# Second attention of a two-layer block: its stages one slot closer together, and the small VectorE steps at other places in a slot

## The chip, the cores and the metric

The kernel runs on one core of a Trainium2 chip. The time is that of one execution on the device, in microseconds (us). The engines are named PE (TensorE), DVE (VectorE), ACT (ScalarE), POOL (GpSimd) and SP (SyncE, which here only issues DMAs).

## The reference

A block of two layers over x of 4 x 1024 tokens by 128. Around two attentions stand four feed-forward layers. The change is in the second attention, which computes two softened sums for each head and adds them:

```python
Q, K, V = (proj(Wq, bq), proj(Wk, bk), proj(Wv, bv))
S = jnp.einsum('bhnd,bhmd->bhnm', Q, K) / dh ** 0.5
W_tau = jax.nn.softmax(S, axis=-1)
W_sigma = 1.0 / ((1.0 + jnp.abs(S) / b_) ** 2 + t_ ** 2)
W_sigma = W_sigma / W_sigma.sum(axis=-1, keepdims=True)
tau = jnp.einsum('bhnm,bhmd->bhnd', W_tau, V)...
sigma = jnp.einsum('bhnm,bhmd->bhnd', W_sigma, V)...
f = 0.5 * tau + 0.5 * sigma
y = f @ Wo.T + bo
```

There are 4 batches of 16 heads, so 64 heads of 1024 x 1024 scores with 8 values a token.

## The kernel before

The function `attend_both` runs through the 64 heads in 256 slots. A head takes four slots; a slot holds two tiles (i = 0 and 1) of 128 rows by 1024 scores. It is a pipeline written out by hand: in slot j each engine works on the slots j, j - LS, j - LT and so on, and the lags LS, LT, LE, LP say how far behind the maxima each stage stands. Sixteen slots are unrolled in the body of a loop. The order on an engine is the order of the code in its `body(it, j)`; engines meet by semaphores alone.

What the engines do in slot j:

- PE computes scores into the PSUM tiles `pm` (for the row maxima, slot j), `pb` (for tau, slot j - LT) and `pa` (for sigma, slot j - LS), each two matmuls of 512 columns at L1951. `weigh` (L1969) multiplies finished weights by the values, eight matmuls, and sums a head in `po`. Once a head the eight columns of maxima are turned into rows (L2011), and the evicted `po` is turned in four pieces (L2026); both go to the PSUM tile `ptr`.
- DVE takes the maximum of `pm` (L2119), the absolute value of `pa` into the SBUF tile `sg` (L2130, an AND on the bits), for i = 0 and i = 1. Then it squares the last quarter of `sg` (L2137: (|s| + b) |s|, both inputs in SBUF). Once a head `negated` writes minus the turned maxima as two bfloat16 rows (L2080, then L2083, both read `ptr`), which SP sends by DMA into the stack of Q (L1924), so that the tau scores come out with their maximum subtracted. And once a head `output` takes reciprocals (L2097), multiplies (L2102, `ptr` by `rz` into `fw`) and adds (L2106, two slices of `fw` into F, which lies in the tile `XNT`; both inputs and the output are in SBUF).
- POOL squares the first three quarters of `sg`: L1898 (tensor_scalar, `sg` + b into `shifted`, which lies in the tile `f0w`) and L1901 (tensor_tensor, `sg` times `shifted`). L1898 waits until both absolute values of its slot are done.
- ACT computes exp for tau (L2044, twice a slot), then for sigma the logarithm (L2053) and the exponential of its negative (L2057), and once a head it evicts `po` into `osb` (L2063).

At the start the sigma work of the slots 0 to 3 is done early, in slots 0 to 3; in the slots from 4 to LS + 3 only maxima (and from slot LT on tau) are done. The tau scores of a head wait for its rows of maxima.

The wait that ties POOL to DVE, and DVE's last steps in a slot:

```python
pool.wait_ge(abs_done, 2 * s + 2)
...
nc.vector.scalar_tensor_tensor(buf[:, :, CUT:T], buf[:, :, CUT:T],
                               parh[:, ring(j, ls), 0:1], buf[:, :, CUT:T],
                               ALU.add, ALU.mult).then_inc(sq_dve, 1)
...
negated(it, j, 0, 1)
output(it, j, 2, LP + 3)
```

Of the kernel before, what the change touches and what calls it, by code (L numbers as in the profile page):

```python
# [15 lines left out]
P = 128  # L16
# [5 lines left out]
HEADS = B * H  # L22
# [1774 lines left out]
def attend_both(nc, tag, V, F, par, qd, kd, ident, stacks, scratch, stack_in):  # L1797
# [5 lines left out]
    SLOTS = HEADS * TT // 2  # L1803
    PER = TT // 2
    UNROLL = PER * RING
    LS, LT, LE, LP = 5, 7, 7, 8
    EARLY = 4
    SC = DH ** -0.5
    CUT = 49 * T // 64
# [1 line left out]
    with ExitStack() as ctx:  # L1811
# [55 lines left out]
        def slots(eng, body):  # L1867
            for j in range(UNROLL):
                body(0, j)
            with eng.Fori(1, SLOTS // UNROLL) as it:  # L1870
                for j in range(UNROLL):
                    body(it, j)
            for j in range(LP + 4):
                body(SLOTS // UNROLL, j)

        def some(x, least=1):
# [3 lines left out]
        with nc.Block() as block:  # L1880
# [64 lines left out]
            @block.tensor  # L1945
            def _(pe):
                pe.wait_ge(vh_cleared, 1)

                def scores(out, lhsT, rhs, t, rows_, sem):
                    for lo in range(0, T, CH):  # L1950
                        last = nc.tensor.matmul(out[:, lo:lo + CH], lhsT[0:rows_, t * P:(t + 1) * P],  # L1951
                                                rhs[0:rows_, lo:lo + CH], start=True, stop=True)
                    last.then_inc(sem, 1)

                def weigh(it, j, s, i):

                    lag = LP + i
                    h, k, r = head(it, j, lag), (j - lag) % PER, (j - lag) % 4
                    t = 2 * k + i
                    if i == 0:  # L1960
                        pe.wait_ge(tau_exp, 2 * s + 2)
                        pe.wait_ge(sig_done, s + 1)
                    if t == 0:
                        pe.wait_ge(head_in[ring(j, lag)], HEAD_LOADS * rounds(it, j, lag))
                        if some(h):
                            pe.wait_ge(o_sb, h)
                    values = Vh[:, ring(j, lag), t * (DH + 1):t * (DH + 1) + 32]
                    for q, (wts, half) in enumerate(((pt[r], 0), (pt[r], 1), (sg[r], 0), (sg[r], 1))):
                        last = nc.tensor.matmul(po[32 * q:32 * q + 32, :], values,  # L1969
                                                wts[:, i, half * CH:(half + 1) * CH],  # L1970
                                                start=(t == 0), stop=(t == TT - 1))
                    last.then_inc(pv_done, 1)

                def body(it, j):
                    sm, st = at(it, j, 0), at(it, j, LT)
                    ss, ls = at_sigma(it, j, LS, 0)
                    rm, rs, rt = (((j - lag) // PER) % RING for lag in (0, ls, LT))
                    if sm is not None and j % PER == 0:
                        pe.wait_ge(stack_in[rm], STACK_LOADS * (it + 1))
                    if st is not None and (j - LT) % PER == 0:  # L1980
                        pe.wait_ge(rows_in[rt], ROW_LOADS * rounds(it, j, LT))
                    for i in range(2):
                        if sm is not None:
                            top = pm
                            if not spare_abs(it, j):
                                if some(2 * sm + i):
                                    pe.wait_ge(max_red, 2 * sm + i)
                            elif j > EARLY:
                                pe.wait_ge(max_red, 2 * sm + i - 1)
                                top = (pm, pa)[i]  # L1990
                            elif i == 0:
                                pe.wait_ge(max_red, 2 * sm)
                            else:
                                pe.wait_ge(abs_done, 2 * EARLY)
                                top = pa
                            scores(top, Q[rm], K[rm], 2 * (j % PER) + i, 96, max_mm)
                        if st is not None:
                            if some(2 * st + i):
                                pe.wait_ge(tau_exp, 2 * st + i)
                            scores(pb, K[rt], Q[rt], 2 * ((j - LT) % PER) + i, P, tau_mm)  # L2000
                        if ss is not None:
                            if some(2 * ss + i):
                                pe.wait_ge(abs_done, 2 * ss + i)
                            scores(pa, K[rs], Q[rs], 2 * ((j - ls) % PER) + i, 96, abs_mm)
                        if i == 1 and j % PER == 0 and at(it, j, 1) is not None:

                            h = head(it, j, 1)
                            pe.wait_ge(max_red, TT * h + TT)
                            if some(h, 3):
                                pe.wait_ge(f_done, h - 2)  # L2010
                            nc.tensor.transpose(ptr[0:TT, 0:P], mx[:, ((j - 1) // PER) % 2, :], ident[:])\  # L2011
                                .then_inc(rows_turned, 1)
                        sp_ = at(it, j, LP + 1 - i)
                        if sp_ is not None:
                            weigh(it, j, sp_, 1 - i)
                    if (j - LP - 2) % PER == PER - 1 and at(it, j, LP + 2) is not None:

                        h = head(it, j, LP + 2)
                        pe.wait_ge(o_sb, h + 1)
                        if isinstance(h, int) and h + 3 > HEADS:  # L2020
                            pe.wait_ge(rows_sb, HEADS)
                            pe.wait_ge(f_done, h)
                        else:
                            pe.wait_ge(rows_sb, h + 3)
                        for c in range(4):
                            last = nc.tensor.transpose(ptr[:, c * P:(c + 1) * P], osb[:, c * P:(c + 1) * P],  # L2026
                                                       ident[:])
                        last.then_inc(o_turned, 1)

                slots(pe, body)  # L2030

            @block.scalar
# [35 lines left out]
            def _(dve):  # L2068
# [40 lines left out]
                def body(it, j):  # L2109
                    sm = at(it, j, 0)  # L2110
                    ss, ls = at_sigma(it, j, LS, 0)
                    for i in range(2):
                        if sm is not None:
                            top = pa if i == 1 and spare_abs(it, j) else pm
                            t = 2 * (j % PER) + i
                            dve.wait_ge(max_mm, 2 * sm + i + 1)
                            if i == 0 and j % PER == 0 and some(sm, 2 * PER):
                                dve.wait_ge(rows_turned, head(it, j, 0) - 1)
                            nc.vector.tensor_reduce(mx[:, (j // PER) % 2, t:t + 1], top[:], AX.X, ALU.max)\  # L2119
                                .then_inc(max_red, 1)  # L2120
                        if i == 0:
                            negated(it, j, 1, 2)
                            output(it, j, 0, LP + 3)
                        else:
                            output(it, j, 1, LP + 3)
                        if ss is not None:
                            dve.wait_ge(abs_mm, 2 * ss + i + 1)
                            if some(ss, 4):
                                dve.wait_ge(pv_done, 2 * (ss - 4) + i + 1)
                            nc.vector.tensor_scalar(sg[(j - ls) % 4][:, i, :].bitcast(I32), pa[:].bitcast(I32),  # L2130
                                                    SIGN_OFF, None, ALU.bitwise_and).then_inc(abs_done, 1)
                    if ss is not None:
                        buf = sg[(j - ls) % 4]
                        dve.wait_ge(abs_done, 2 * ss + 2)
                        if (j - ls) % PER == 0:
                            dve.wait_ge(head_in[ring(j, ls)], HEAD_LOADS * rounds(it, j, ls))
                        nc.vector.scalar_tensor_tensor(buf[:, :, CUT:T], buf[:, :, CUT:T],  # L2137
                                                       parh[:, ring(j, ls), 0:1], buf[:, :, CUT:T],
                                                       ALU.add, ALU.mult).then_inc(sq_dve, 1)
                    negated(it, j, 0, 1)  # L2140
                    output(it, j, 2, LP + 3)

                slots(dve, body)
        m.clear_sems()
# [155 lines left out]
```

## Time and profile before

| | |
|---|---|
| time before, median of 3 runs | 2910.45 us (2909.16 to 2911.09) |
| the profiled execution | 2910.0 us, of which the span 2908.2 us |
| PE, DVE busy over the span | 2446.8 us (84%), 2437.5 us (84%) |
| ACT, POOL busy over the span | 2255.8 us (78%), 1998.7 us (69%) |
| second attention | first maximum at 1156.35 us, last add at 2633.88 us |

The span is the time from the first to the last instruction of one profiled execution. Busy times are sums of the recorded instructions of an engine; on ACT and DVE a record can overlap its neighbour by some hundredths to some tenths of a microsecond, since the next instruction is already let in. So the time that an instruction costs its engine is the distance from its start to the start of the next, and the record's length is the time until its result is there.

### The profile page before, as it was taken

How to read it: one execution, taken by the hardware profiler on the slowest of the kernel's cores; microseconds unless marked ns; L12 is line 12 of the kernel's file. 1: busy time of each engine (PE TensorE's matmuls, PEld its weight loads, DVE VectorE, ACT ScalarE, POOL GpSimd, SP SyncE). 2: the span in 40 equal slices, each digit the busy share in tenths (PEclk: the TensorE clock that was granted, in tenths of full speed). 3: DMA queues.
4: the chain of work that ended last, by engine and by line, in shares of the span. 5: the costliest groups of instructions: out<-in, count | busy, mean ns of one | idle time of the engine just before them, and what ended most of it. 6: DMA issues, size and time to landing. Idle time of an engine off the chain costs nothing. (4 is left out here: it accounts for less than half of the span.)

```text
span 2908.2 us, 60009 instructions
## 1 busy us (share of the span) xinstructions
PE 2446.8 (84%) x18487; PEld 1013.1 (35%) x18614; DVE 2437.5 (84%) x3916; ACT 2255.8 (78%) x2521; POOL 1998.7 (69%) x1255
## 2 busy tenths in 40 slices
PE   2657999998577996899998999999999999983898
PEld 2643333334465663122222222222222222222566
DVE  4667888885577656999999999999999999986765
ACT  4464777776455555799999999999999999992554
POOL 4532222222454654799999999999999999993455
PEclk9977999999687997799999999999999999996799
DMA  3232100000120002000000000000000000000000
GB/s 117 70 92 71 29 29 28 28 29 8 50 81 1 1 0 100 15 15 15 14 18 14 14 14 16 16 14 14 15 17 14 14 14 17 15 1 1 1 11 18
DMA packets 93503, 76.57 MB, mean 26 GB/s; under 512 B 32480, under 2 KB 73960, under 8 KB 93264
## 3 DMA queue, kind: packets, MB, share of 16 engines
q1 hardware_dynamic: 89104, 66.36, 7.8%
q0 software_dynamic: 4288, 8.82, 0.9%
q8 instruction: 58, 0.95, 0.1%
q14 instruction: 53, 0.43, 0.1%
HBM read 47.77 MB, written 24.42 MB: 25 GB/s over the span
## 5 line engine op out<-in xcount | busy, mean ns | idle before, releaser
L1901 POOL TENSOR_TENSOR a_sg<-a_sg,all_f0w 128x1568 f32<-128x1568 f32 x256 | 904.9, 3535 | 21.4
L2044 ACT ACTIVATE a_pt<-a_pb 128x1024 f32<-128x1024 f32 x512 | 702.7, 1372 | 12.1 <-PE a_pb L1951 12.1
L2119 DVE TENSOR_REDUCE a_mx<-a_pm 128x1 f32<-128x1024 f32 x507 | 613.8, 1211 | 11.4 <-PE a_pm L1951 10.0
L2130 DVE TENSOR_SCALAR a_sg<-a_pa 128x1024 int32<-128x1024 int32 x512 | 615.6, 1202 | 8.5 <-PE a_pa L1951 8.3
L2053 ACT ACTIVATE a_sg<-a_sg,a_parh 128x2048 f32<-128x2048 f32 x256 | 602.2, 2352 | 15.3 <-POOL a_sg L1901 15.3
L1969 PE MATMUL a_po<-a_pt,a_Vh 128*32 128x512 f32 x2048 | 541.2, 607 | 64.7 <-ACT a_osb L2063 62.5
L2057 ACT ACTIVATE a_sg<-a_sg 128x2048 f32<-128x2048 f32 x256 | 581.2, 2270 | 0.1
L1969 PE MATMUL a_po<-a_sg,a_Vh 128*32 128x512 f32 x2048 | 541.1, 607 | 0.0
L1898 POOL TENSOR_SCALAR all_f0w<-a_sg,a_parh 128x1568 f32<-128x1568 f32 x256 | 513.6, 2006 | 30.0 <-DVE a_sg L2130 27.1
L1711 ACT ACTIVATE a_pt<-a_ring 128x1024 f32<-128x1024 f32 (+2 forms) x384 | 313.6, 846 | 150.4 <-PE a_ring L1638 147.1
L1783 DVE TENSOR_REDUCE a_mx<-a_ring 128x2 f32<-128x1024 f32 (+3 forms) x384 | 359.1, 955 | 74.0 <-PE a_ring L1621 55.1
L1951 PE MATMUL a_pm<-all_K,all_Q 96*128 96x512 bf16 x1014 | 312.2, 390 | 44.9 <-DVE a_mx L2119 33.8
L1552 POOL TENSOR_SCALAR_AFFINE_SELECT a_pt<-a_pt 128x256 f32<-128x256 f32 x256 | 104.0, 406 | 355.6 <-ACT a_pt L1711 355.2
L1951 PE MATMUL a_pa<-all_Q,all_K 96*128 96x512 bf16 x1024 | 311.1, 385 | 10.5 <-DVE a_sg L2130 1.5
L1951 PE MATMUL a_pb<-all_Q,all_K 128*128 128x512 bf16 x897 | 281.1, 383 | 28.0 <-ACT a_pt L2044 17.7
L2137 DVE SCALAR_TENSOR_TENSOR a_sg<-a_sg,a_parh 128x480 f32<-128x480 f32 x256 | 218.7, 854 | 10.6
L1951 PEld LDWEIGHTS a_pm<-all_K,all_Q 96*128 96x128 bf16 x1014 | 63.1, 98 | 428.2 <-DVE a_mx L2119 362.3
L895 ACT ACTIVATE f_sg<-f_psg 128x512 f32<-128x512 f32 x176 | 104.5, 594 | 117.1 <-PE f_psg L854 117.1
L1655 PE MATMUL a_po<-a_pt,a_Vh 128*32 128x384 f32 (+3 forms) x1920 | 191.4, 437 | 1.9 <-POOL a_pt L1552 1.8
L1969 PEld LDWEIGHTS a_po<-a_pt,a_Vh 128*32 128x32 f32 x2048 | 75.9, 108 | 280.4 <-issue 260.6
L949 DVE TENSOR_TENSOR f_su<-f_psu,f_sg 128x512 f32<-128x512 f32 x144 | 98.7, 687 | 79.4 <-PE f_psu L854 74.0
L1638 PE MATMUL a_ring<-all_Q,all_K 50*128 50x512 bf16 (+2 forms) x768 | 132.1, 342 | 37.9 <-DVE a_mx L1783 33.1
(283 smaller groups left out, 4585.2 us busy)
## 6 DMA issues: line engine op xcount, KB each, us to landing
all_Q<-q_parts SPq DMA_DIRECT2D x256, 48.0 KB
all_K<-k_parts SPq DMA_DIRECT2D x256, 48.0 KB
k_parts<-p_parts SPq DMA_DIRECT2D x16, 384.0 KB, 3.1
e_recs<-routed_rows SPq DMA_DIRECT2D x70, 64.5 KB, 1.9
all_Q<-a_rows SPq DMA_DIRECT2D x256, 2.0 KB
q_parts<-p_parts SPq DMA_DIRECT2D x16, 192.0 KB, 2.4
q_parts<-p_parts SPq DMA_DIRECT2D x8, 384.0 KB, 2.6
a_Vh<-all_V SPq DMA_DIRECT2D x64, 36.0 KB, 1.8
```

The source lines that it names most:

```text
L1711: nc.scalar.activation(pt[n % 4][:, :, ga:gb, c * P:CH], of_weight(y)[:, :, 0:(gb - ga) * width].rearrange("p u (g n) -> p u g n", n=width ...
L1783: nc.vector.tensor_reduce(mx[:, j % 2, half, :, strip_at(t)], of_maximum(y)[:, :, 0:min(CH, (t + 1) * P - half * CH)], AX.X, ALU.max).then ...
L1898: nc.gpsimd.tensor_scalar(sums, buf[:, :, 0:CUT], b2, 1.0, ALU.add, ALU.mult)\
L1901: nc.gpsimd.tensor_tensor(buf[:, :, 0:CUT], buf[:, :, 0:CUT], sums, ALU.mult)\
L1951: last = nc.tensor.matmul(out[:, lo:lo + CH], lhsT[0:rows_, t * P:(t + 1) * P], rhs[0:rows_, lo:lo + CH], start=True, stop=True)
L1969: last = nc.tensor.matmul(po[32 * q:32 * q + 32, :], values, wts[:, i, half * CH:(half + 1) * CH], start=(t == 0), stop=(t == TT - 1))
L2044: nc.scalar.activation(pt[(j - LT) % 4][:, i, :], pb[:], ACT.Exp, scale=SC)\
L2053: nc.scalar.activation(buf[:], buf[:], ACT.Ln, bias=parh[:, ring(j, le), 1:2]).then_inc(ln_done, 1)
L2057: nc.scalar.activation(buf[:], buf[:], ACT.Exp, scale=-1.0).then_inc(sig_done, 1)
L2119: nc.vector.tensor_reduce(mx[:, (j // PER) % 2, t:t + 1], top[:], AX.X, ALU.max)\
L2130: nc.vector.tensor_scalar(sg[(j - ls) % 4][:, i, :].bitcast(I32), pa[:].bitcast(I32), SIGN_OFF, None, ALU.bitwise_and).then_inc(abs_done, 1)
L2137: nc.vector.scalar_tensor_tensor(buf[:, :, CUT:T], buf[:, :, CUT:T], parh[:, ring(j, ls), 0:1], buf[:, :, CUT:T], ALU.add, ALU.mult).then_ ...
```

## The change

All four lags are one slot shorter. The maxima of a head are turned on PE one half slot earlier, right behind the scores of i = 0, and the two negated rows are written behind the first and the second absolute values of that slot. The four turns of the output stand on PE ahead of a `weigh` instead of behind it. The three output steps on DVE are spread anew: the reciprocal at the end of a slot, the multiply and the add in the two halves of the next one. One slot more is run at the end, since the last output steps are one slot further behind LP.

```diff
-    LS, LT, LE, LP = 5, 7, 7, 8
+    LS, LT, LE, LP = 4, 6, 6, 7
...
-            for j in range(LP + 4):
+            for j in range(LP + 5):
                 body(SLOTS // UNROLL, j)
...
-                        if i == 1 and j % PER == 0 and at(it, j, 1) is not None:
+                        if i == 0 and j % PER == 0 and at(it, j, 1) is not None:
...
+                        if i == 0 and (j - LP - 3) % PER == PER - 1 and at(it, j, LP + 3) is not None:
+
+                            h = head(it, j, LP + 3)
+                            pe.wait_ge(o_sb, h + 1)
...
+                            for c in range(4):
+                                last = nc.tensor.transpose(ptr[:, c * P:(c + 1) * P], osb[:, c * P:(c + 1) * P],
+                                                           ident[:])
+                            last.then_inc(o_turned, 1)
                         sp_ = at(it, j, LP + 1 - i)
                         if sp_ is not None:
                             weigh(it, j, sp_, 1 - i)
-                    if (j - LP - 2) % PER == PER - 1 and at(it, j, LP + 2) is not None:
...
                         if i == 0:
-                            negated(it, j, 1, 2)
-                            output(it, j, 0, LP + 3)
+                            output(it, j, 1, LP + 4)
                         else:
-                            output(it, j, 1, LP + 3)
+                            output(it, j, 2, LP + 4)
                         if ss is not None:
                             dve.wait_ge(abs_mm, 2 * ss + i + 1)
...
                                                     SIGN_OFF, None, ALU.bitwise_and).then_inc(abs_done, 1)
+                        negated(it, j, i, 1)
...
-                    negated(it, j, 0, 1)
-                    output(it, j, 2, LP + 3)
+                    output(it, j, 0, LP + 3)
```

Line numbers of the changed kernel are one or two lower: the maximum is L2118, the absolute values L2128, the squares L2136, the reciprocal L2096, the multiply L2101, the add L2105, the negated rows L2079 and L2082, the turn of the output L2023.

On DVE, in the slot of the loop that holds the multiply, the order before is this (`a_fw` is written by the multiply and read by the add, `a_sg` by the squares):

```order
L2097 RECIPROCAL a_rz<-a_ptr 128x16
L2130 TENSOR_SCALAR a_sg<-a_pa 128x1024
L2116 REGISTER_ALU
L2119 TENSOR_REDUCE a_mx<-a_pm 128x1
L2102 TENSOR_TENSOR a_fw<-a_ptr,a_rz 128x128
L2130 TENSOR_SCALAR a_sg<-a_pa 128x1024
L2137 SCALAR_TENSOR_TENSOR a_sg<-a_sg,a_parh 128x2x240
L2106 ISA
L2106 TENSOR_TENSOR all_XNT<-a_fw 128x8x8
L2116 ISA
L2119 TENSOR_REDUCE a_mx<-a_pm 128x1
```

In the changed kernel the same slot, from the squares of the slot before to its own squares, reads:

```order
L2136 SCALAR_TENSOR_TENSOR a_sg<-a_sg,a_parh 128x2x240
L2096 RECIPROCAL a_rz<-a_ptr 128x16
L2115 ISA
L2118 TENSOR_REDUCE a_mx<-a_pm 128x1
L2101 TENSOR_TENSOR a_fw<-a_ptr,a_rz 128x128
L2128 TENSOR_SCALAR a_sg<-a_pa 128x1024
L2115 REGISTER_ALU
L2118 TENSOR_REDUCE a_mx<-a_pm 128x1
L2105 ISA
L2105 TENSOR_TENSOR all_XNT<-a_fw 128x8x8
L2128 TENSOR_SCALAR a_sg<-a_pa 128x1024
L2136 SCALAR_TENSOR_TENSOR a_sg<-a_sg,a_parh 128x2x240
```

The add stood behind the squares, with the next slot's maximum after it; it now stands between the second maximum and the second absolute values of the slot.

The first slot of a head on DVE in the changed kernel, where the maxima of the head before are turned (`a_rows` are the negated rows):

```order
L2079 TENSOR_SCALAR a_rows<-a_ptr 8x128
L2115 REGISTER_ALU
L2118 TENSOR_REDUCE a_mx<-a_pm 128x1
L2128 TENSOR_SCALAR a_sg<-a_pa 128x1024
L2082 SCALAR_TENSOR_TENSOR a_rows<-a_ptr,a_rows 8x128
L2135 ISA
L2136 SCALAR_TENSOR_TENSOR a_sg<-a_sg,a_parh 128x2x240
```

Before, L2080 stood at the end of that slot, behind the squares, and L2083 behind the first maximum of the next one; now the second row is written between the absolute values and the squares.

## Rows read from the trace of the kernel before

**Rows 1.** Windows: us, busy us of PE, PEld, DVE, ACT, POOL, clock, DMA.

```profile
1420.00:2560.00 1140.00, 1041.62 (x5825) 266.12 (x5924) 1130.15 (x1267) 1140.00 (x861) 1118.35 (x406) 1.00 0.05 15
```

**Rows 2.** Timeline of ACT: start us, length us, engine, line; two evictions in a row.

```profile
2004.46 1.01 ACT L2063 ACTIVATE a_osb<-a_po 128x512 f32<-128x512 f32 x1
...
2027.01 1.01 ACT L2063 ACTIVATE a_osb<-a_po 128x512 f32<-128x512 f32 x1
```

**Rows 3.** L2044 by its line: durations in ns, min/median/max, first and last start.

```profile
L2044 ACT ACTIVATE a_pt<-a_pb x512: 1006/1408/1457, 1187.3 to 2625.5; 128x1024 f32<-128x1024 f32 x171
```

**Rows 4.** Timeline of DVE over the slot that holds the add.

```profile
1988.31 1.20 DVE L2130 TENSOR_SCALAR a_sg<-a_pa 128x1024 int32<-128x1024 int32 x1
1989.65 0.72 DVE L2137 SCALAR_TENSOR_TENSOR a_sg<-a_sg,a_parh 128x480 f32<-128x480 f32 x1
1990.29 1.21 DVE L2119 TENSOR_REDUCE a_mx<-a_pm 128x1 f32<-128x1024 f32 x1
1991.43 0.24 DVE L2097 RECIPROCAL a_rz<-a_ptr 128x16 f32<-128x16 f32 x1
1991.59 1.16 DVE L2130 TENSOR_SCALAR a_sg<-a_pa 128x1024 int32<-128x1024 int32 x1
...
1993.80 0.27 DVE L2102 TENSOR_TENSOR a_fw<-a_ptr,a_rz 128x128 f32<-128x128 f32 x1
1993.99 1.21 DVE L2130 TENSOR_SCALAR a_sg<-a_pa 128x1024 int32<-128x1024 int32 x1
1995.24 0.72 DVE L2137 SCALAR_TENSOR_TENSOR a_sg<-a_sg,a_parh 128x480 f32<-128x480 f32 x1
1995.87 0.21 DVE L2106 TENSOR_TENSOR all_XNT<-a_fw 128x64 f32 x1
```

**Rows 5.** Timeline of POOL over the same slot.

```profile
1989.68 2.04 POOL L1898 TENSOR_SCALAR all_f0w<-a_sg,a_parh 128x1568 f32<-128x1568 f32 x1 [0.20 <-DVE a_sg L2130]
1991.81 3.52 POOL L1901 TENSOR_TENSOR a_sg<-a_sg,all_f0w 128x1568 f32<-128x1568 f32 x1
1995.37 2.07 POOL L1898 TENSOR_SCALAR all_f0w<-a_sg,a_parh 128x1568 f32<-128x1568 f32 x1
```

**Rows 6.** Timeline of DVE and POOL in the output projection: L1384 free, then beside L1344.

```profile
2648.58 0.17 DVE L1384 TENSOR_TENSOR o_t<-o_t,o_ve 128x8 f32<-128x8 f32 x1
...
2670.78 2.33 POOL L1344 TENSOR_TENSOR all_X<-all_X,all_lb 128x1024 f32<-128x1024 f32 x1
...
2670.87 2.26 DVE L1384 TENSOR_TENSOR o_t<-o_t,o_ve 128x8 f32<-128x8 f32 x1
```

**Rows 7.** Timeline near the end of the attention: L1901, and the squares beside it.

```profile
2589.19 3.51 POOL L1901 TENSOR_TENSOR a_sg<-a_sg,all_f0w 128x1568 f32<-128x1568 f32 x1
...
2591.68 1.54 DVE L2137 SCALAR_TENSOR_TENSOR a_sg<-a_sg,a_parh 128x480 f32<-128x480 f32 x1
```

**Rows 8.** L2106 and L1898 by their lines: durations in ns, min/median/max.

```profile
L2106 DVE TENSOR_TENSOR all_XNT<-a_fw x64: 212/218/224, 1229.8 to 2633.9; 128x64 f32 x60, 128x64 f32<-128x64 f32 x4
...
L1898 POOL TENSOR_SCALAR all_f0w<-a_sg,a_parh x256: 1932/1995/2077, 1161.2 to 2615.7; 128x1568 f32<-128x1568 f32 x128
```

**Rows 9.** The page's groups: busy us, mean ns, idle us before them.

```profile
L1898 POOL TENSOR_SCALAR all_f0w<-a_sg,a_parh 128x1568 f32<-128x1568 f32 x256 | 513.6, 2006 | 30.0 <-DVE a_sg L2130 27.1
```

**Rows 10.** Timeline of POOL: L1898 of slot 0 and of slot 4.

```profile
1161.23 2.02 POOL L1898 TENSOR_SCALAR all_f0w<-a_sg,a_parh 128x1568 f32<-128x1568 f32 x1 [6.01 <-DVE a_sg L2130]
...
1201.47 1.93 POOL L1898 TENSOR_SCALAR all_f0w<-a_sg,a_parh 128x1568 f32<-128x1568 f32 x1 [18.02 <-DVE a_sg L2130]
```

**Rows 11.** Timeline while the pipeline fills: the second negated row, and PE behind its DMA.

```profile
1181.93 0.27 DVE L2083 SCALAR_TENSOR_TENSOR a_rows<-a_ptr,a_rows 8x128 bf16<-8x128 f32 x1
...
1184.74 1.04 PE L1951 MATMUL a_pm<-all_K,all_Q 96*128 96x512 bf16 x2 [0.31 <-DMA all_Q<-a_rows]
```

**Rows 12.** Timeline at the end: the last L1901 and the last logarithm.

```profile
2617.73 3.54 POOL L1901 TENSOR_TENSOR a_sg<-a_sg,all_f0w 128x1568 f32<-128x1568 f32 x1
...
2623.63 2.08 ACT L2053 ACTIVATE a_sg<-a_sg,a_parh 128x2048 f32<-128x2048 f32 x1
```

More of the change, by code:

```diff
@@ L2012, in body @@
                                 .then_inc(rows_turned, 1)
+                        if i == 0 and (j - LP - 3) % PER == PER - 1 and at(it, j, LP + 3) is not None:
+                            h = head(it, j, LP + 3)
+                            pe.wait_ge(o_sb, h + 1)
+                            if isinstance(h, int) and h + 3 > HEADS:
+                                pe.wait_ge(rows_sb, HEADS)
+                                pe.wait_ge(f_done, h)
+                            else:
+                                pe.wait_ge(rows_sb, h + 3)
+                            for c in range(4):
+                                last = nc.tensor.transpose(ptr[:, c * P:(c + 1) * P], osb[:, c * P:(c + 1) * P],
+                                                           ident[:])
+                            last.then_inc(o_turned, 1)
                         sp_ = at(it, j, LP + 1 - i)
@@ L2015, in body @@
                             weigh(it, j, sp_, 1 - i)
-                    if (j - LP - 2) % PER == PER - 1 and at(it, j, LP + 2) is not None:
[L2018 to L2028, printed above, removed]
                 slots(pe, body)
```

## Prediction

> **What bounds the kernel now.** I first read the page's busy shares, which say little here since they mix ten stages, and then the stretch of the second attention by windows [rows 1]. The attention runs from about 1155 to 2634 us. Between 1420 and 2560 us, where nothing starts or ends, ACT is busy 1140.00 of 1140 us, DVE 1130.15, POOL 1118.35 and PE 1041.62, at full granted clock. Three engines are full at once, so I had to find out which one sets the pace, and how far the others may slip.
>
> ACT does. One head (four slots) takes 22.55 us from one eviction of `po` to the next [rows 2]. An exponential L2044 takes 1006 ns at its shortest and 1408 ns at its median [rows 3]; the work is the same each time, so I read the 0.4 us as waiting behind the instruction ahead. ACT is never short of work in the steady part, and small slips of the others are caught by these 0.4 us.
>
> Then DVE and POOL, row by row over one slot [rows 4, 5]. DVE has no gap: maximum, absolute values, maximum, absolute values, each 1.13 us after the last, then the squares L2137. POOL has a gap of 0.20 us once in this piece; otherwise L1901 and L1898 follow each other. L1898 waits for the second absolute values of its slot. So POOL has almost no reserve: what comes late on DVE ahead of that instruction costs POOL time.
>
> The third thing to see is how DVE and POOL block each other. In the output projection a tiny DVE instruction with both inputs in SBUF, L1384 on 128x8, took 2.26 us where 0.17 us is its free length [rows 6]. It began at 2670.87, 0.09 us after POOL's tensor_tensor L1344, and ended at 2673.13; L1344 ended at 2673.11. Such a DVE instruction waits for the end of POOL's tensor_tensor. Inside the attention the squares L2137 show it too: 0.72 us free, 1.54 us at 2591.68, ended at 2593.22, which is 0.52 us after L1901 ended at 2592.70 [rows 7]. DVE instructions that read PSUM don't wait: L2102 took 0.27 us at 1993.80 in the middle of an L1901 that lasted from 1991.81 to 1995.33 [rows 4, 5].
>
> **The change, part by part.**
>
> *The output add (L2106 before).* It adds two slices of `fw`, both in SBUF, and writes SBUF: the form that waits. Today it stands right behind the squares. There it starts at 1995.87, when L1901 has ended (1995.33), and takes 0.21 us [rows 4, 5]; over 64 instances it is 212 to 224 ns [rows 8]. The change puts it in the second half of the slot, between the maximum and the absolute values (the second piece of order in the section on the change). Where is L1901 then? In today's rows of this very slot the squares of the slot before start at 1989.65 and are followed 0.64 us later. Put in the new order from there: reciprocal 1990.29, maximum 1990.46, multiply 1991.59, absolute values 1991.79, maximum 1992.92, add 1994.05 (0.17 us for the reciprocal, 0.20 for the multiply, 1.13 for each of the others: the differences of starts in rows 4). L1901 runs from 1991.81 to 1995.33 [rows 5]. The add lands 2.2 us into it and 1.3 us before its end, further from both ends than any shift of phase seen here. It waits for the end.
>
> Behind the add, in order on DVE, stand the absolute values of this slot, and POOL's next L1898 waits for those. So POOL goes idle, and DVE cannot make it good earlier, since DVE is itself tied to the end of L1901 by the squares. The idle time of POOL per head: the absolute values start about 0.03 us around the end of L1901 (a waiting instruction ends 0.02 us after POOL's, and the next starts 0.08 us before that end, as 1990.29 behind 1989.65 + 0.72); they take 1.20 us; L1898 starts 0.17 us after their end (1989.68 against 1988.31 + 1.20) [rows 4, 5, 6]. That is 1.37 us. Absolute values stand behind the add for heads 0 to 61 (the add of head h is in slot 4h + 14, the last absolute values in slot 259): 62 x 1.37 = **+84.9 us**. Bounds for one, with 0.1 us of doubt on how closely the three follow each other: 1.25 and 1.45.
>
> *POOL's waits of today.* L1898 waited 30.0 us in all, of which 6.01 at the start and 18.02 in the filling [rows 9, 10]. The other 6.0 us are waits like the 0.20 above, ahead of the first absolute values of a head. With POOL held once a head, DVE runs ahead in the other slots and these go: **-6.0 us** (bound: nothing). L1898 is 1932 to 2077 ns [rows 8], and I take its longer records for the share of the add and the squares beside it; the add leaves it, which I estimate at 0.03 us a head: **-2 us**, between -6 and +2.
>
> *One lag less, at the start.* One slot with maxima alone goes, but the first tau scores need the row of maxima. PE waited for this DMA, then began slot 7 at 1184.74; the second half of the rows was written from 1181.93, so the way takes 2.8 us [rows 11]. In the new order it stands behind the second maximum of slot 4, one maximum (1.13 us) earlier. Slot 6, which is the first with tau scores then, begins at some 1183.6 and takes the place of slot 7: **-1.1 us**.
>
> *The end.* Today ACT is behind: the last L1901 ends at 2621.27, its logarithm starts at 2623.63 [rows 12]. With ACT no longer full it can start right then: **-2.3 us**, between 0 and -2.4.
>
> *Edits costed at nothing.* The negated rows are the same two instructions, both reading PSUM and so not held by POOL, moved by about half a slot. Outside the slot of the add DVE has over 1 us a head of slack then; without it they could cost what they last, 0.27 us each [rows 11]. The turn of the maxima and the four turns of the output on PE move ahead of a `weigh`. PE waits 98.4 of the 1140 us [rows 1], which is 1.9 us a head (50.6 heads), and gets 1.2 us more; were that cover gone, a few tenths a head would reach DVE's second maximum.
>
> *ACT as a floor.* POOL's head becomes 22.55 + 1.2 = 23.8 us, above ACT's 22.55, so nothing of the 1.37 us is hidden by ACT; PE waits too.
>
> Sum: 84.9 - 6.0 - 2 - 1.1 - 2.3 = +73.5 us. The profiled execution took 2910.0 us (span 2908.2), which gives 2983.5; the median shown is 2910.45, so 2984 against it.
>
> **A rule weighed.** In the 64 rows of L2106 POOL's L1898 is recorded as running (1995.37 to 1997.44 around 1995.87), and the add takes 0.21 us all the same [rows 4, 5, 8]. The Trainium skill, on the page SBUF — State Buffer, section "Who interferes with whom", says that a DVE instruction with two SBUF inputs contends with a GpSimd instruction that reads SBUF, and that the second to issue fully blocks. Taken by recorded starts it would make each of today's adds wait some 1.6 us, and these rows do not; by the rows the add is free behind the squares and held by L1901, and by the rule it would be held in both places, so that the change would add nothing; that outcome is rival A's. The measured rows decide for me: the squares, which start first, seem to hold POOL's L1898, and the add follows in their shelter.
>
> **The rivals.**
> *A, the add isn't held* (the change is then neutral). For: its neighbourship with L1898 cost it nothing 64 times. Against: rows 6 and 7, the same form against the same POOL instruction. Then ACT keeps the pace, and only the -1.1 us at the start is left: 2909 us. It decides where the hold is under some 0.1 us a head.
> *B, faster.* As A, and POOL's 6.0 us of waits turn into time: 2910.45 - 6.0 - 1.1 = 2903 us. Against: ACT is full [rows 1 to 3], so it cannot use them.
> *C, slower still.* The second negated row now stands between the absolute values and the squares of the first slot of a head. If L1898 gets in first and holds the squares for its own work (about 1.4 us, from the squares' end to its end: 1995.96 to 1997.44), the squares end some 1.3 us later, of which DVE's lead takes 0.3 us, and POOL loses about 1 us more a head: 2984 + 62 = 3046 us. The squares would start some 0.12 us after the absolute values, L1898 0.17 us; today one slot in 16 has 0.14 and 0.17 (1989.65 and 1989.68 against 1989.51) and the squares took 0.72 us there [rows 4, 5]. It decides where the squares start after L1898.
>
> **How the numbers follow.** The add held: 0.84. A: 0.09. B: 0.03. C: 0.04. The forecast is the first case's time, 2984 us. Its range: at the low end 62 x 1.25 - 6 - 6 - 1.1 - 2.4 = 62, at the high end 62 x 1.45 + 2 - 1.1 = 91, with the present waits kept and nothing given back at the end. On 2910 us that is 2972 to 3001, rounded to 2970 and 3000. It leaves out A, B and C, 0.16 in all, and little of the first. A change within 0.2% (5.8 us) can't be told from none in this kernel. Faster by more: B, 0.03. Within: A, 0.09. Slower: 0.88.
>
> **What the changed profile would show.** The add (L2105 then) at 1.2 to 1.6 us on average instead of 0.22, each ending within 0.1 us of an end of L1901; POOL's idle time ahead of L1898 at about 110 us, put down to DVE's absolute values; a head 23.8 us from one eviction of `po` to the next; L2043 near 1.0 us, no longer 1.4. An add of 0.22 us in the middle of L1901 makes the prediction wrong (A); squares of over 2 us once a head mean C.

## The result, and the profile after

The changed kernel takes 2982.18 us (median of 4 runs, 2977.1 to 2982.58), beside 2909.8 us for the kernel before, measured along with it (4 runs, 2907.73 to 2911.09): 1.0244 times as long, 95% interval 1.0232 to 1.0256. It is slower by 72 us. The prediction was 2984 us and slower. The profiled execution took 2981.99 us, of which the span is 2980.2 us: 72.0 us more than before in both.

The page's groups of the changed kernel (busy us, mean ns, idle us before them) show where the time stands:

```profile
L1898 POOL TENSOR_SCALAR all_f0w<-a_sg,a_parh 128x1568 f32<-128x1568 f32 x256 | 509.5, 1990 | 110.4 <-DVE a_sg L2128 107.6
L2043 ACT ACTIVATE a_pt<-a_pb 128x1024 f32<-128x1024 f32 x512 | 523.8, 1023 | 57.4 <-PE a_pb L1951 51.9
```

POOL's idle time ahead of L1898 rose from 30.0 us [rows 9] to 110.4 us. ACT's exponential fell from 1408 ns at the median [rows 3] to 1024 ns: it hardly waits behind the instruction ahead any more.

The window in the middle, with the columns of [rows 1]:

```profile
1420.00:2560.00 1140.00, 1002.88 (x5620) 259.02 (x5616) 1134.85 (x1201) 1103.96 (x817) 1057.29 (x385) 1.00 0.05 14
```

DVE's busy time even rose, 1130.15 to 1134.85 us, though it starts fewer instructions (1201 in place of 1267). The record of a held instruction counts as busy, so DVE's busy share says nothing of the work done here; the counts do. The other engines lost busy time.

The lines of the add, the squares and L1898 (ns, min/median/max; below L1898 its waits, in us and times):

```profile
L2105 DVE TENSOR_TENSOR all_XNT<-a_fw x64: 224/1520/3607, 1233.3 to 2706.7; 128x64 f32 x60, 128x64 f32<-128x64 f32 x4
...
L2136 DVE SCALAR_TENSOR_TENSOR a_sg<-a_sg,a_parh x256: 696/940/2474, 1160.7 to 2688.8; 128x480 f32<-128x480 f32 x128
...
L1898 POOL TENSOR_SCALAR all_f0w<-a_sg,a_parh x256: 1967/1982/2037, 1160.8 to 2690.7; 128x1568 f32<-128x1568 f32 x128
...
  DVE a_sg L2128: 107.6, 62
```

The add went from a median of 218 ns [rows 8] to 1520 ns. The 62 waits in the last line are not yet those of the 62 heads whose add has absolute values behind it: they hold the wait of 6.01 us at the start and the one of 18.25 us in the filling. In the timeline of POOL the other 60 are of 1.38 or 1.39 us each, and two more of the same length (2.8 us together), at the first and at the last of these heads, are put down to "issue". That makes one wait for each of the 62 heads. The slot of one add on DVE (start us, length us), which answers to [rows 4]:

```profile
1705.98 0.27 DVE L2101 TENSOR_TENSOR a_fw<-a_ptr,a_rz 128x128 f32<-128x128 f32 x1
1706.18 1.21 DVE L2128 TENSOR_SCALAR a_sg<-a_pa 128x1024 int32<-128x1024 int32 x1
1707.31 1.21 DVE L2118 TENSOR_REDUCE a_mx<-a_pm 128x1 f32<-128x1024 f32 x1
1708.44 1.51 DVE L2105 TENSOR_TENSOR all_XNT<-a_fw 128x64 f32 x1
1709.87 1.21 DVE L2128 TENSOR_SCALAR a_sg<-a_pa 128x1024 int32<-128x1024 int32 x1
1711.12 0.72 DVE L2136 SCALAR_TENSOR_TENSOR a_sg<-a_sg,a_parh 128x480 f32<-128x480 f32 x1
```

And POOL beside it, as in [rows 5]:

```profile
1706.34 3.53 POOL L1901 TENSOR_TENSOR a_sg<-a_sg,all_f0w 128x1568 f32<-128x1568 f32 x1
1711.25 2.02 POOL L1898 TENSOR_SCALAR all_f0w<-a_sg,a_parh 128x1568 f32<-128x1568 f32 x1 [1.39 <-DVE a_sg L2128]
```

The add starts 2.10 us into L1901 and ends at 1709.95, 0.08 us after L1901 (1709.87). The absolute values start at 1709.87 and end at 1711.08; L1898 starts 0.17 us later, after 1.39 us of idle. The two timelines together tell the cause: the wait is put down to the absolute values, which took their usual 1.21 us, so it is their start that is late, and what stands ahead of them is the add.

### The profile page after: what moved, and what is told of

Read it like the earlier page. It is cut to its first block and busy times, and to the rows that moved or that the text cites. A ratio compares the mean times of both kernels' runs of the same rounds, so it can differ in the third digit from the quotient of the medians.

```text
span 2980.2 us, 60091 instructions
## 1 busy us (share of the span) xinstructions
PE 2463.6 (83%) x18614; PEld 1018.0 (34%) x18614; DVE 2522.2 (85%) x3916; ACT 2283.3 (77%) x2521; POOL 1994.1 (67%) x1255
## 5 line engine op out<-in xcount | busy, mean ns | idle before, releaser
L1901 POOL TENSOR_TENSOR a_sg<-a_sg,all_f0w 128x1568 f32<-128x1568 f32 x256 | 904.5, 3533 | 21.4
L2118 DVE TENSOR_REDUCE a_mx<-a_pm 128x1 f32<-128x1024 f32 x508 | 611.2, 1203 | 13.2 <-PE a_pm L1951 13.2
L2128 DVE TENSOR_SCALAR a_sg<-a_pa 128x1024 int32<-128x1024 int32 x512 | 618.6, 1208 | 2.0 <-PE a_pa L1951 2.0
L1898 POOL TENSOR_SCALAR all_f0w<-a_sg,a_parh 128x1568 f32<-128x1568 f32 x256 | 509.5, 1990 | 110.4 <-DVE a_sg L2128 107.6
L2043 ACT ACTIVATE a_pt<-a_pb 128x1024 f32<-128x1024 f32 x512 | 523.8, 1023 | 57.4 <-PE a_pb L1951 51.9
L2052 ACT ACTIVATE a_sg<-a_sg,a_parh 128x2048 f32<-128x2048 f32 x256 | 512.2, 2001 | 15.3 <-POOL a_sg L1901 15.3
L2056 ACT ACTIVATE a_sg<-a_sg 128x2048 f32<-128x2048 f32 x256 | 487.6, 1905 | 0.1
L1951 PE MATMUL a_pb<-all_Q,all_K 128*128 128x512 bf16 x1024 | 307.6, 381 | 7.2 <-ACT a_pt L2043 7.2
L2136 DVE SCALAR_TENSOR_TENSOR a_sg<-a_sg,a_parh 128x480 f32<-128x480 f32 x256 | 226.6, 885 | 6.9
L1951 PEld LDWEIGHTS a_pa<-all_Q,all_K 96*128 96x128 bf16 x1024 | 68.8, 97 | 322.8 <-DVE a_sg L2128 313.5
```

Of the source, the lines that this page charges most:

```text
L1898: nc.gpsimd.tensor_scalar(sums, buf[:, :, 0:CUT], b2, 1.0, ALU.add, ALU.mult)\
L1901: nc.gpsimd.tensor_tensor(buf[:, :, 0:CUT], buf[:, :, 0:CUT], sums, ALU.mult)\
L2043: nc.scalar.activation(pt[(j - LT) % 4][:, i, :], pb[:], ACT.Exp, scale=SC)\
L2052: nc.scalar.activation(buf[:], buf[:], ACT.Ln, bias=parh[:, ring(j, le), 1:2]).then_inc(ln_done, 1)
L2056: nc.scalar.activation(buf[:], buf[:], ACT.Exp, scale=-1.0).then_inc(sig_done, 1)
```

## The experiments

My theory was that the whole loss is the held add: a DVE instruction with two SBUF inputs that comes while POOL works on SBUF waits for POOL's end, and the absolute values queued behind it come late for POOL. Against it stood: that the shorter lags, the moved turns or the moved rows cost something too; that the add waits for another reason than its two SBUF inputs; and, for the add of before, that it is free beside L1898 because a tensor_scalar holds nothing, rather than because the squares hold L1898.

### The add put back behind the squares, the rest of the change kept

```diff
-                        else:
-                            output(it, j, 2, LP + 4)
...
+                    output(it, j, 2, LP + 4)
                     output(it, j, 0, LP + 3)
```

> The changed kernel with the add alone put back behind the squares of its slot; lags, turns, negated rows, reciprocal and multiply stay as changed. Theory H (the add is held by POOL's tensor_tensor, and that is the whole loss): the add takes 0.22 us again, POOL's 62 waits of 1.39 us go (86 us), ACT keeps the pace with 22.55 us a head, and the time is 2909 us (2907 to 2911), some 0.4 to 1.1 us under the kernel before from the earlier start. Rival R (part of the 72 us lies with the turns ahead of the weighing, the rows or the lags): the time stays above 2915 us by that part, with DVE waiting for the scores on PE.

2909.51 us (11 runs) beside 2909.62 us for the kernel before (21 runs): ratio 0.9999, interval 0.999 to 1.0008, as expected. The lines of its add and its tau exponential:

```profile
L2105 DVE TENSOR_TENSOR all_XNT<-a_fw x64: 209/213/224, 1236.9 to 2633.2; 128x64 f32 x60, 128x64 f32<-128x64 f32 x4
...
L2043 ACT ACTIVATE a_pt<-a_pb x512: 1006/1397/1557, 1188.5 to 2625.8; 128x1024 f32<-128x1024 f32 x171
```

The add is free again and ACT is full again (its exponential at 1397 ns). So the place of one instruction of 0.2 us is the whole loss, and the lags, the turns on PE and the moved rows together are worth nothing that can be told from none here, within some 3 us by the interval.

### The kernel before, with its add moved into the second half

This is the converse: of the whole change, only the add's move, on the old lags.

```diff
                             output(it, j, 1, LP + 3)
+                            output(it, j, 2, LP + 3)
...
                     negated(it, j, 0, 1)
-                    output(it, j, 2, LP + 3)
```

> The kernel before with the add alone moved, from behind the squares to behind the multiply, in the middle of L1901. Theory H: every add lasts until L1901 ends, POOL waits 1.39 us a head for heads 0 to 61, +86 us, less 6 us of today's waits and 2.3 us at the end: 2986 us (2978 to 2992). Rival R: the time stays near 2910 us, and the loss needs the shorter lags.

2987.94 us (4 runs): ratio 1.0267, interval 1.0251 to 1.0283, inside the expected 2978 to 2992. Its add and the waits of its L1898 (the start and the filling are two of the 62 again):

```profile
L2106 DVE TENSOR_TENSOR all_XNT<-a_fw x64: 224/1289/1394, 1226.3 to 2710.5; 128x64 f32 x60, 128x64 f32<-128x64 f32 x4
...
  DVE a_sg L2131: 107.1, 62
```

The record of the add is shorter here (1289 ns, since it starts later within L1901), but POOL's wait is the same: 1.39 us a head. The length of the held record is not the price. In both kernels every add held in the middle of L1901 ends 0.08 or 0.09 us after it, and the price is what has to follow from there before POOL can go on: the absolute values and the hand-over.

### The add with one input from PSUM, at its new place

```diff
                         tau, sigma = (fw[:, :, 2 * k:2 * k + 2].rearrange("p c s d -> p s c d") for k in range(2))
+                        tau = o[:, :, 0:2, 0:DH].rearrange("p c s d -> p s c d")
```

It leaves out the product of the first part with its reciprocals; the instruction's size, place and output stay.

> The changed kernel with the add at its new place, but its first input read from the PSUM tile ptr, so that one input alone is in SBUF. The product of the first part with its reciprocal sums is left out of the result. Theory H: a DVE instruction with one SBUF input is not held; 0.22 to 0.30 us in the middle of L1901, no waits of POOL, 2909 us (2906 to 2911). Rival P (it is the place, or the write to SBUF, that is held by POOL): the add stays at 1.5 us and the time at 2982 us.

2907.94 us (10 runs): ratio 0.9996, interval 0.9987 to 1.0005, as expected. The timeline of DVE at one add:

```profile
2021.86 0.21 DVE L2106 TENSOR_TENSOR all_XNT<-a_ptr,a_fw 128x64 f32 x1
2021.99 1.21 DVE L2129 TENSOR_SCALAR a_sg<-a_pa 128x1024 int32<-128x1024 int32 x1
```

and POOL at that time:

```profile
2019.76 3.55 POOL L1901 TENSOR_TENSOR a_sg<-a_sg,all_f0w 128x1568 f32<-128x1568 f32 x1
```

In the same place, 2.1 us into L1901, with the same output in SBUF, it takes 0.21 us (204 to 225 ns over all 64). The second SBUF input makes the wait, neither the place alone nor the write.

### The add between the second absolute values and the squares

Here the add delays the squares: they are recorded 0.24 us after the end of the absolute values, in place of 0.04 us in the changed kernel's slot above, so that L1898 comes first. This tells more on why the add of before was free.

```diff
                         if i == 0:
                             output(it, j, 1, LP + 4)
-                        else:
-                            output(it, j, 2, LP + 4)
...
                         negated(it, j, i, 1)
+                    output(it, j, 2, LP + 4)
                     if ss is not None:
```

> The changed kernel with the add behind the second absolute values, ahead of the squares. POOL's next L1898 no longer waits for anything behind the add. The add is held to the end of L1901 (0.4 to 0.6 us), and L1898 starts at that end, while the squares are still behind the add. Theory L (L1898 holds the squares too once it has started first): squares of about 2 us once a head, DVE late by about 1.3 us, POOL waiting 0.3 to 1.2 us a head: 2925 to 2975 us. Theory S (L1898 with one SBUF input does not hold them): squares of 0.7 to 1.0 us and 2909 us.

2988.23 us (4 runs): ratio 1.0263, interval 1.0245 to 1.028. L1898 does hold the squares, so theory L stands, but the time lies above its 2925 to 2975 us. DVE around one add:

```profile
2020.00 1.21 DVE L2126 TENSOR_SCALAR a_sg<-a_pa 128x1024 int32<-128x1024 int32 x1
2021.13 0.40 DVE L2105 TENSOR_TENSOR all_XNT<-a_fw 128x64 f32 x1
2021.45 2.05 DVE L2135 SCALAR_TENSOR_TENSOR a_sg<-a_sg,a_parh 128x480 f32<-128x480 f32 x1
```

and POOL:

```profile
2015.84 1.97 POOL L1898 TENSOR_SCALAR all_f0w<-a_sg,a_parh 128x1568 f32<-128x1568 f32 x1
...
2021.43 1.57 POOL L1898 TENSOR_SCALAR all_f0w<-a_sg,a_parh 128x1568 f32<-128x1568 f32 x1
...
2028.20 2.02 POOL L1898 TENSOR_SCALAR all_f0w<-a_sg,a_parh 128x1568 f32<-128x1568 f32 x1 [1.33 <-DVE a_sg L2126]
```

Look at the two lengths of L1898. At 2021.43 it starts 0.02 us before the squares and lasts 1.57 us; the squares, free at 0.72 us, last 2.05 and end at 2023.50, 0.50 us after it. At 2015.84 and 2028.20 the squares started first, and it lasts 1.97 to 2.02 us. It is so in all 62 heads: L1898 lasts 1.56 to 1.60 us where it is recorded first, 1.97 to 2.10 us elsewhere. So L1898 holds the squares, and where they are first the squares hold L1898; the 0.4 us that each of the 256 has more in the kernel before [rows 8] is waiting, recorded as its own time. The changed kernel shows it in a second way. In all its 256 slots L1898 ends 1.44 to 1.46 us after the squares end, though it starts anywhere from 0.13 to 1.94 us after they start. It goes by their end and not by its own start.

That explains the add of before in part. DVE had L1898 stopped when the add came right behind the squares, and the add went in ahead of it. It was nearly free: L1898 ends 1.49 us after the squares in the 62 slots with an add behind them, 1.44 us at the median in the other 194. But to stand right behind another such instruction is not always shelter. Here the squares stand right behind the add, which itself waited for L1901, and L1898, recorded 0.02 to 0.05 us ahead of them, went first in all 62 heads. What decides between the two cases no run shows.

The squares end 1.33 us later than free, and in the slot after POOL waits 1.32 to 1.52 us, 61 times. The expectation had put this wait at 0.3 to 1.2 us. And 20 waits of 0.56 to 0.81 us (14.6 us) come one slot later, where DVE waits for PE's scores: each follows on a fall of PE's granted clock to 0.50 (0.97 over the middle window, where the changed kernel has 1.00).

### The add one half slot earlier

The multiply moves along, to stay ahead of the add.

```diff
                         if i == 0:
-                            output(it, j, 1, LP + 4)
-                        else:
                             output(it, j, 2, LP + 4)
...
                     output(it, j, 0, LP + 3)
+                    output(it, j, 1, LP + 3)
```

The add comes right at the start of L1901, so the hold lasts nearly all of it, with three instructions behind it in place of one.

> The changed kernel with multiply and add one half slot earlier: multiply behind the reciprocal at the slot's end, add behind the first maximum of the next slot. Theory Q (what counts is what is queued on DVE behind the held add until POOL gets its next input): the add lasts about 3.6 us, and behind the end of L1901 come the absolute values, the maximum and the absolute values again, 2 x 1.13 us more than before, so POOL waits 1.39 + 2.26 = 3.65 us a head, 62 x 2.26 = 140 us over the changed kernel: 3122 us (3110 to 3135). Rival T (a hold costs POOL a fixed time, wherever the add stands in L1901): 2982 us.

3188.12 us (4 runs): ratio 1.0975, interval 1.0957 to 1.0992. That is 66 us above the expected 3122 and outside its range. DVE over one such slot and into the next (the squares left out):

```profile
2001.65 3.57 DVE L2105 TENSOR_TENSOR all_XNT<-a_fw 128x64 f32 x1
2005.14 1.21 DVE L2126 TENSOR_SCALAR a_sg<-a_pa 128x1024 int32<-128x1024 int32 x1
2006.28 1.21 DVE L2118 TENSOR_REDUCE a_mx<-a_pm 128x1 f32<-128x1024 f32 x1
2007.57 1.23 DVE L2126 TENSOR_SCALAR a_sg<-a_pa 128x1024 int32<-128x1024 int32 x1
...
2010.32 1.22 DVE L2118 TENSOR_REDUCE a_mx<-a_pm 128x1 f32<-128x1024 f32 x1 [0.77 <-PE a_pm L1951]
2012.13 1.22 DVE L2126 TENSOR_SCALAR a_sg<-a_pa 128x1024 int32<-128x1024 int32 x1 [0.59 <-PE a_pa L1951]
```

and POOL:

```profile
2001.63 3.51 POOL L1901 TENSOR_TENSOR a_sg<-a_sg,all_f0w 128x1568 f32<-128x1568 f32 x1
2008.97 2.02 POOL L1898 TENSOR_SCALAR all_f0w<-a_sg,a_parh 128x1568 f32<-128x1568 f32 x1 [3.83 <-DVE a_sg L2126]
...
2016.12 2.02 POOL L1898 TENSOR_SCALAR all_f0w<-a_sg,a_parh 128x1568 f32<-128x1568 f32 x1 [1.53 <-DVE a_sg L2126]
```

POOL loses 3.83 us (3.65 forecast), the three instructions that stand between the end of L1901 and L1898. That part came as the theory has it. The second wait, 1.53 us a slot later, did not stand in it. Windows of four microseconds, with the columns of [rows 1], show its origin (the clock is the third column from the end):

```profile
2004.00:2008.00 4.00, 1.59 (x6) 0.33 (x10) 3.91 (x4) 2.25 (x2) 1.14 (x1) 0.65 0.01 5
2008.00:2012.00 4.00, 4.00 (x18) 0.82 (x14) 2.74 (x3) 0.74 (x1) 2.94 (x2) 0.50 0.00 0
```

While DVE was held (to 2005.14) and POOL then waited (to 2008.97) PE had little to do (1.59 of 4 us), its granted clock fell to 0.50, the level of 1.2 GHz, and its scores then came too late for DVE, which waited 0.77 and 0.59 us. Of POOL's waits in this execution 53 are of 3.65 to 3.84 us (198.2 us in sum), as the theory has them, and 68 are of under 3 us (63.5 us), as the one at 2016.12. Together they are 261.7 us, in place of 86.1 us in the changed kernel. That is 175.6 of the 187.9 us by which this execution (3169.87 us, the shortest of the four) is longer than the changed kernel's; the rest is not accounted for. The theory had 62 waits of 3.65 us, 226 us. So the second waits are more than the 48 us by which this execution passed 3122, and the heads without such a hold took a part back.

These are 8 heads in which the add came right at L1901's start, like the others, and was not held, for example at 1979.02 (L1901 recorded from 1979.01):

```profile
1979.02 0.21 DVE L2105 TENSOR_TENSOR all_XNT<-a_fw 128x64 f32 x1
1979.15 1.22 DVE L2126 TENSOR_SCALAR a_sg<-a_pa 128x1024 int32<-128x1024 int32 x1
```

To the hundredth of a microsecond the two kinds look alike. By the nanoseconds of the kept trace the eight free adds start 12 to 16 ns after L1901's recorded start, and the 53 held ones 16 to 22 ns after it. A few nanoseconds of the records separate 0.21 from 3.6 us, and they overlap at 16.

### Half of the eviction left out

To see whether ACT sets the pace when nothing is held, ACT evicts only half of the columns of `po`; the rest of the output is left out, filled with ones once at the start. The add stands behind the squares.

```diff
-                            nc.scalar.activation(osb[:], po[:], ACT.Copy).then_inc(o_sb, 1)
+                            nc.scalar.activation(osb[:, 0:CH // 2], po[:, 0:CH // 2], ACT.Copy).then_inc(o_sb, 1)
```

> The kernel with the add behind the squares (e1), in which ACT evicts only half the columns of po into osb once a head; the other half of the result is left out (it is filled with ones at the start). It takes some 0.21 us a head from ACT and nothing from DVE or POOL. Theory A (ACT keeps the pace once the add is free, and that is why the shorter lags gain nothing): a head falls from 22.55 us until POOL holds at about 22.4, 0.15 to 0.2 us a head: 2897 to 2901 us. Rival D (DVE and POOL keep the pace, ACT only looks full): 2909 us.

2895.95 us (5 runs) beside 2907.13 us for the kernel before, which the kernel of the first experiment equals: ratio 0.9956, interval 0.9942 to 0.9969, 1 us under the expected 2897 to 2901. Two evictions in a row, and the middle window:

```profile
2000.97 0.43 ACT L2063 ACTIVATE a_osb<-a_po 128x256 f32<-128x256 f32 x1
2023.34 0.40 ACT L2063 ACTIVATE a_osb<-a_po 128x256 f32<-128x256 f32 x1
```

```profile
1420.00:2560.00 1140.00, 1058.67 (x5968) 280.52 (x5967) 1134.55 (x1276) 1139.99 (x867) 1122.99 (x409) 1.00 0.05 15
```

A head takes 22.37 us in place of 22.55: less work on ACT is less time, as the reading of [rows 1 to 3] has it. But it is only 0.2 us a head. POOL (1122.99 of 1140 us, up from 1118.35 in [rows 1]) and DVE (1134.55) stand right behind ACT (1139.99): three engines are within 1.5% of full. The tau exponential fell to 1067 ns at the median, so ACT now waits hardly at all behind its own queue. Which of the three sets the pace then, no run shows.

## Why the prediction was right, and where it was not

**The held add: right.** Forecast 1.37 us a head and 62 of them; measured 1.38 to 1.39 us and 62. The steps were as predicted: the add starts 2.1 us into L1901 (2.2 forecast) and lasts 1.51 us, within the 1.2 to 1.6 given; a head takes 23.75 us (23.8). The first two experiments show that the add's place makes the whole loss, the third that its second SBUF input is what the place acts on.

**POOL's waits of before, -6.0 us: right.** The idle time ahead of L1898 is 110.4 us; 6.01 and 18.25 us of it are the start and the filling, and 86.1 us the 62 waits. Nothing is left over, so the 6.0 us have gone. (The prediction reads them all as waits like the one of 0.20 us; 13 such waits make 3.1 us of them, and the rest are gaps of under 0.15 us, spread over many slots.)

**L1898, -2 us: the right sign, too small.** Its busy time fell from 513.6 [rows 9] to 509.5 us: -4.1, inside the bounds of -6 and +2. The picture, that the add makes these records longer, holds: 1.49 in place of 1.44 us after the squares' end, 0.05 us a head where 0.03 was put, so 3.1 us of the 4.1. What it missed is that all 256 records contain some 0.4 us of waiting for the squares.

**The start, -1.1 us: wrong.** The step that failed is that slot 6, with its first tau scores, begins at some 1183.6 and takes the place of slot 7. PE did start it early, in the changed kernel:

```profile
1183.20 1.03 PE L1951 MATMUL a_pm<-all_K,all_Q 96*128 96x512 bf16 x2 [1.64 <-DMA all_Q<-a_rows]
...
1187.97 1.04 PE L1951 MATMUL a_pb<-all_Q,all_K 128*128 128x512 bf16 x2 [2.04 <-ACT a_pt L2043]
```

This is 1.54 us before [rows 11], of which 0.42 us are the earlier start of the attention (first maximum at 1155.93, in place of 1156.35), and 1.12 the forecast gain. But the timeline of ACT in the changed kernel shows what it was busy with:

```profile
1183.06 2.00 ACT L2052 ACTIVATE a_sg<-a_sg,a_parh 128x2048 f32<-128x2048 f32 x1 [1.59 <-POOL a_sg L1901]
...
1186.91 1.01 ACT L2043 ACTIVATE a_pt<-a_pb 128x1024 f32<-128x1024 f32 x1
```

ACT still did the last early sigma work, in program order ahead of the first tau exponential, and PE's next scores waited 2.04 us for that. In the kernel before ACT has the same two instructions there:

```profile
1183.49 2.00 ACT L2053 ACTIVATE a_sg<-a_sg,a_parh 128x2048 f32<-128x2048 f32 x1 [1.61 <-POOL a_sg L1901]
...
1187.34 1.01 ACT L2044 ACTIVATE a_pt<-a_pb 128x1024 f32<-128x1024 f32 x1
```

From the first maximum to the first tau exponential it is 30.99 us before (1156.35 to 1187.34) and 30.98 us after (1155.93 to 1186.91). I followed the chain on PE and never looked at what ACT does then: the gain of 1.1 us lay beside other work. POOL got nothing of it either: L1898 of slot 4 starts 45.35 us after the first maximum (1201.28), 45.12 us before [rows 10]. The term -1.1 is worth nothing, and at this place +0.2.

**The end, -2.3 us: right.** The timelines of POOL and ACT in the changed kernel:

```profile
2692.70 3.53 POOL L1901 TENSOR_TENSOR a_sg<-a_sg,all_f0w 128x1568 f32<-128x1568 f32 x1
```

```profile
2696.27 2.00 ACT L2052 ACTIVATE a_sg<-a_sg,a_parh 128x2048 f32<-128x2048 f32 x1
```

The logarithm starts 0.04 us after the last L1901 ends (2696.23), in place of 2.36 us [rows 12].

The sum: POOL's idle time +80.4, L1898 -4.1, the end -2.3 make +74.0, and the span grew by 72.0. Of the 2.0 us between them 0.4 lie ahead of the first maximum and 0.6 behind the start of the last logarithm; the rest I did not follow up, and it is under what two executions of one kernel differ by.

**The rule weighed: the rule was right and my reading of it was not.** I took POOL's record, which begins before the add of before, for a hold, and so had the rule speak for rival A. The experiment with the add ahead of the squares shows that the record begins while the squares still hold the instruction: 2.0 us recorded for 1.57 of work. By that, the second to issue is fully blocked, and the second was L1898. The Trainium skill's page SBUF — State Buffer, section "Who interferes with whom", says so ("Issue order, not op shape, decides who blocks"), and the traces agree in both directions: squares of 2.05 us in place of 0.72 behind L1898, and L1898 of 1.97 to 2.10 us in place of 1.57 behind the squares. What this doesn't answer is why the add, the third to come, went ahead of the L1898 that already waited. The guess of a shelter, which I had from the rows, fits the kernel before and the first experiment, and it does not hold for the squares behind a held add.

**The rivals.** A (not held) fell with the add at 1520 ns; the experiment with the input from PSUM shows what it would have looked like. B fell with it. C (the second negated row lets L1898 in ahead of the squares) did not happen in the changed kernel: in the first slot of a head the squares start 0.13 us after the absolute values have ended, L1898 0.27 us after (1201.14 and 1201.28 in slot 4, the values' end at 1201.01). It was near. In the variant with the input from PSUM, which has the same negated rows, it happened in one head:

```profile
2079.62 2.15 DVE L2137 SCALAR_TENSOR_TENSOR a_sg<-a_sg,a_parh 128x480 f32<-128x480 f32 x1
```

```profile
2079.70 1.57 POOL L1898 TENSOR_SCALAR all_f0w<-a_sg,a_parh 128x1568 f32<-128x1568 f32 x1
...
2086.47 2.02 POOL L1898 TENSOR_SCALAR all_f0w<-a_sg,a_parh 128x1568 f32<-128x1568 f32 x1 [1.34 <-DVE a_sg L2129]
```

The squares are recorded 0.08 us ahead of L1898 and were held all the same, so the order of the recorded starts is not safe proof of who came first. POOL's next L1898 waited 1.34 us, against the 1 us that the prediction set for C.

## What to carry to other kernels

A small DVE instruction with both inputs in SBUF costs next to nothing or much by its neighbours: right behind squares that had stopped POOL it went through (0.21 us), in the middle of a long POOL tensor_tensor it waits for that one's end. Its price is then not its own wait but the work queued behind it up to the next hand-over to the engine that has no reserve: one instruction made 1.4 us a head, three made 3.7 to 3.8. Before such a step is moved, write down what POOL does at that time, and give it a PSUM input where the data allow it. And where an earlier start of one engine is to be worth something, follow every engine that the first result needs, not only the one that was waiting.

## What the hardware showed that I had not expected

- POOL's tensor_scalar L1898 holds DVE's squares as its tensor_tensor does: 0.72 us became 2.05 (the add ahead of the squares). And a held POOL instruction shows as a long one, not as a gap: 1.57 us of work recorded as 1.97 to 2.04 in all 256 of the changed kernel.
- At the start of a POOL instruction some nanoseconds decide: the add there took 0.21 us in 8 heads (recorded 12 to 16 ns after L1901) and 3.6 us in 53 others (16 to 22 ns; the add one half slot earlier).
- Waits of 3.8 us in the pipeline were followed by falls of PE's granted clock from 1.00 to 0.50 for some microseconds, and these by a second wait in the next slot. In the changed kernel, with 1.39 us a head, the clock of the middle window stayed at 1.00. The length of the wait alone doesn't tell: with the add ahead of the squares POOL waits 1.33 us a head and the clock fell too, to 0.97 over the window.
- ACT's eviction L2062 lasts 0.59 us in the changed kernel and 1.01 us before [rows 2], with the same operands. Like the exponential's 1.02 and 1.41 us, I read the difference as waiting behind its queue; both go together as a sign of whether ACT is full.
